# Moving the end of self-attention into cross-attention's first steps, and splitting the experts' weight loads, in a one-core decoder layer

## The reference

```
x = x + bitlinear(self_attention(quantised q, k, v of layernorm(x)), wo, go)
x = x + cross_attention(layernorm(x), context)         # 16 heads of 128, q and k rms-normalised
x = x + experts(layernorm(x))                          # 8 experts, top 2, 688 hidden, silu gate

bitlinear(x, w, g): x/rms(x)*g rounded to 8 bits per token, w rounded to -1, 0, 1
experts: probs = softmax(top 2 of x @ router_w.T)
         y = (silu(x @ gate.T) * (x @ up.T)) @ down.T, summed over the two with probs
```

## Time and profile before

| | us |
|---|---|
| median of 3 runs | 933.92 (932.38 to 935.29) |
| the profiled execution | 935.83 |
| its span, first to last instruction | 934.0 |
| PE busy | 792.0 (85%) |
| DVE busy | 628.4 (67%) |
| ACT busy | 537.2 (58%) |
| POOL busy | 385.2 (41%) |

### The profile page before, as it was taken

How to read it: one execution, slowest core, us unless ns; L and a number is a source line. 1 busy time by engine, 2 the same in 40 slices (tenths; PEclk the granted TensorE clock), 3 DMA queues, 4 the chain that set the end, 5 groups by cost and what they waited for, 6 DMA issues and landing times. The chain is left out here.

```text
span 934.0 us, 29446 instructions
## 1 busy us (share of the span) xinstructions
PE 792.0 (85%) x11809; PEld 574.7 (62%) x11809; DVE 628.4 (67%) x1110; ACT 537.2 (58%) x1002; POOL 385.2 (41%) x445
## 2 busy tenths in 40 slices
PE   0599989982998999999999969973989999999992
PEld 0488878861444656566656557651657777777771
DVE  6788999644789999989999989679323333333330
ACT  1687777762777767676767646340435445454450
POOL 0232222131346555555555575102344555555532
PEclk9998999965999999999999998985999999999996
DMA  9110000000463344434343522290682222222224
GB/s 323 52 49 25 26 25 26 26 2 26 145 208 121 119 133 136 123 109 137 93 138 104 157 90 65 71 385 15 253 277 45 41 41 46 37 44 44 38 35 107
DMA packets 59402, 91.97 MB, mean 98 GB/s; under 512 B 6768, under 2 KB 39664, under 8 KB 59088
## 3 DMA queue, kind: packets, MB, share of 16 engines
q1 hardware_dynamic: 48048, 76.26, 24.6%
q0 software_dynamic: 7488, 10.23, 6.8%
q10 hardware_dynamic: 3744, 3.67, 1.1%
HBM read 63.13 MB, written 29.10 MB: 99 GB/s over the span
## 5 line engine op out<-in xcount | busy, mean ns | idle before, releaser
L1565 DVE SCALAR_TENSOR_TENSOR hid<-psu,hid 128x688 f32<-128x688 f32 x39 | 34.1, 875 | 147.4 <-ACT hid L1427 147.4
L1178 PE MATMUL xbank_a<-arena,x_o 128*128 128x256 f16 x768 | 97.9, 279 | 8.5 <-DVE x_o L1003 6.1
L1427 ACT ACTIVATE hid<-psg 128x688 f32<-128x688 f32 x39 | 29.0, 744 | 117.3 <-PE psu L1642 117.3
L1178 PEld LDWEIGHTS xbank_a<-arena,x_o 128*128 128x128 f16 x768 | 72.3, 99 | 29.3 <-DVE x_o L1003 17.4
L1083 PE MATMUL xbank_qk<-arena 128*128 128x512 f16 x336 | 83.5, 385 | 5.0 <-DVE x_gains L988 3.9
L1657 PE MATMUL fbank<-arena,hidT 128*128 (+1 forms) x663 | 84.3, 276 | 0.8 <-ACT f_y L1447 0.8
L849 POOL TENSOR_TENSOR x_pf<-x_sc,x_rden 128x512 f32<-128x512 f32 x32 | 33.4, 1043 | 107.2 <-DVE x_rden L1026 107.2
L1642 PE MATMUL psg<-wgu,f_xT 128*128 x468 | 75.2, 310 | 2.1 <-ACT f_xT L1434 2.1
L1642 PE MATMUL psu<-wgu,f_xT 128*128 x468 | 74.6, 309 | 0.0
L1657 PEld LDWEIGHTS fbank<-arena,hidT 128*128 128x128 f16 (+1 forms) x663 | 63.5, 98 | 16.3 <-issue 9.5
L889 ACT ACTIVATE sqq<-xbank_qk 128x512 f32<-128x512 f32 x56 | 33.4, 597 | 64.5 <-PE xbank_qk L1083 64.5
(11 more groups left out here) (274 smaller groups left out, 2039.8 us busy)
## 6 DMA issues: line engine op xcount, KB each, us to landing
arena<-in_wx SPq DMA_DIRECT2D x51, 256.0 KB, 3.8
wgu<-w_hl SPq DMA_DIRECT2D x8, 1376.0 KB
ao<-key_norms SPq DMA_DIRECT2D x64, 128.0 KB, 3.7
w_hl<-cT SPq DMA_DIRECT2D x26, 256.0 KB, 2.1
w_hl<-x_pair SPq DMA_DIRECT2D x25, 256.0 KB, 3.3
arena<-w_hl SPq DMA_DIRECT2D x8, 384.0 KB
ao<-in_wx SPq DMA_DIRECT2D x10, 256.0 KB, 3.5
w_hl<-ao SPq DMA_DIRECT2D x10, 256.0 KB, 2.6
```

The lines of the kernel that those rows point to most:

```text
L1178: last = nc.tensor.matmul(acc[t // 2][:, (t % 2) * C:(t % 2 + 1) * C], o_hl[h % 2][:, a, at:at + P], wvo[:, b, e, :], start=(e == 0 and j ...
L1565: nc.vector.scalar_tensor_tensor(out=h3, in0=psu[:, :].rearrange("p (c n) -> p c n", c=2)[:, :, 0:FH], scalar=HID_UP / (H_UP * W_UP), in1= ...
```

## The change

Self-attention's loop now ends at t = 15. What was left of pairs 4 to 7 is done in the cross-attention block: a first part ahead of its loop, the rest between the operations of m = 0 to 6. The banks are cross-attention's own, `xbank_s` for turns of zo, the two halves of `xbank_o` for the projection and the turned pairs. The operands (ao2, ug, zo, zoT, hp, h, w_int and others, the tuple `Carry`) lie in slots of k_hl that heads of m = 5 to 8 write first, wvT_raw in slots 0 to 7. `value_weights` and its two splits go from lag 2 to lag 1, so to odd t = 1 to 15. PE's wait for the gains is gone, and ACT's explicit load of its table.

In the experts, SP loads the router's weights first, then the gate and up halves of all eight experts in two DMAs, then saves x, then loads the down weights of three experts; those of the other five wait for the routing. `gate_up` waits only for both gate and up DMAs; `down` waits for its expert.

```diff
-        steps = range(-4, NT + 7)
+        steps = range(-4, NT)
...
-                    if pair(t, 2) is not None:
-                        value_weights(t, pair(t, 2))
+                    if pair(t, 1) is not None:
+                        value_weights(t, pair(t, 1))
...
+                gained_last()
+                rest_low(5)
                 for N in steps:
-                    n = N + 1
+                    n, m = N + 1, N + AHEAD
                     if piece(piece_at(N, 1)):
                         piece_low(piece_at(N, 1))
+                    if m == 3:
+                        rest_low(6)
+                    if m == 5:
+                        rest_low(7)
...
-                nc.scalar.preload_act_table_set("natural_log_exp_and_others")
-                act.wait_ge(g_ready, 4)
...
+                def rest_high(j):
+                    act.wait_ge(h_done, 2 * (j - 4))
+                    act.wait_ge(ht_done, j - 4)
+                    nc.scalar.copy(hp[:, :, 0, :], h_rest[:, :, :]).then_inc(hh_done, 1)
...
+                squares_last()
+                second_norm(5)
+                turned_out(6)
+                rest_high(5)
+                quantise_last()
+                act.wait_ge(g_ready, 3)
...
                     if pair(m):
                         key(2 * m + 1)
+                    if m == 1:
+                        turned_out(7)
+                        second_norm(6)
+                    if m == 2:
+                        rest_high(6)
+                    if m == 3:
+                        second_norm(7)
+                    if m == 4:
+                        rest_high(7)
...
+                second_stats(5)
...
+                turned_hidden(4)
+                hidden(5)
+                scale_last()
+                dve.wait_ge(g_in, 32)
...
                     if pair(m):
                         query_low(2 * m)
                         key_halves(2 * m)
+                    if m == 0:
+                        integers_last()
+                    if m == 1:
+                        second_stats(6)
+                    if m == 2:
+                        hidden(6)
+                    if m == 3:
+                        second_stats(7)
+                    if m == 4:
+                        hidden(7)
...
                     if pair(m):
                         key_halves(2 * m + 1)
+                    if m == 0:
+                        residual_out(6)
+                    if m == 1:
+                        turned_hidden(5)
+                    if m == 2:
+                        residual_out(7)
+                    if m == 4:
+                        turned_hidden(6)
+                    if m == 6:
+                        turned_hidden(7)
...
-                pe.wait_ge(g_ready, 4)
...
+                turn_hidden(4)
+                turn_out(6)
...
                         key(2 * m)
+                    if m == 0:
+                        project_rest(6)
+                    if m == 1:
+                        turn_out(7)
+                    if m == 2:
+                        project_rest(7)
+                    if m == 4:
+                        turn_hidden(6)
+                    if m == 6:
+                        turn_hidden(7)
...
                     if pair(m):
                         squares(2 * m + 1)
+                    if m == 0:
+                        turn_hidden(5)
...
+                sp.dma_start(wr[:, :, :], dram["wr"].rearrange("p (k e) -> p k e", k=NCH)).then_inc(s["wr_in"], 16)
+                for l in range(2):
+                    sp.dma_start(wgu[:, :, l * GUC:(l + 1) * GUC], weights[l, :, :, 0:GUC]).then_inc(s["gate_up_in"], 16)
...
+                down_weights(0, 3)
+                sp.wait_ge(down_in[0], 64)
+                sp.sem_inc(s["experts_in"], 3)
+
+                sp.wait_ge(s["h_saved"], 32)
+                sp.wait_ge(s["routed"], 1)
+                down_weights(3, NE)
...
-                    pe.wait_ge(s["experts_in"], e + 1)
+                    if n == 0:
+                        pe.wait_ge(s["gate_up_in"], 32)
...
                     e = expert_of[n]
+                    pe.wait_ge(s["experts_in"], e + 1)
```

More of the change, by code:

```diff
@@ L2 @@
 from concourse import mybir
+from collections import namedtuple
 from contextlib import ExitStack
@@ L504, in _ @@
                         turned_hidden(pair(t, 8))
-                    if pair(t, 2) is not None:
-                        value_low(pair(t, 2))
+                    if pair(t, 1) is not None:
+                        value_low(pair(t, 1))
                     if tile(t + 1):
@@ new lines, in quantise_last, with turned_out @@
+                def quantise_last():
+                    act.wait_ge(so_done, 2)
+                    for a in range(2):
+                        nc.scalar.activation(ug[:, a, :], ug[:, a, :], ACT.Identity, scale=qsc_o[:, NPAIRS - 1, a:a + 1], bias=cst[:, CONSTS + 5:CONSTS + 6]).then_inc(yo_done, 1)
+                def turned_out(j):
+                    act.wait_ge(zt_done, j - 5)
+                    need(act, wo_done, j - 6)
+                    nc.scalar.copy(zoT[:, :, :, :].rearrange("p a k n -> p (a k n)"), bank_s[:, :].bitcast(BF16)[:, 0:2 * C]).then_inc(zoT_done, 1)
@@ new lines, in integers_last, with residual_out @@
+                def integers_last():
+                    dve.wait_ge(yo_done, 2)
+                    dve.wait_ge(zt_done, 1)
+                    nc.vector.tensor_scalar(zo[:, :, :], ug[:, :, :], MAGIC, None, ALU.subtract).then_inc(zo_done, 1)
+                def residual_out(j):
+                    dve.wait_ge(wo_done, j - 5)
+                    if j == NPAIRS - 1:
+                        dve.wait_ge(so_done, 2)
+                    for a in range(2):
+                        nc.vector.scalar_tensor_tensor(out=x_sb[:, 2 * j + a, :], in0=bank_wo[:, a * C:(a + 1) * C], scalar=deq_o[:, j, a:a + 1],
+                                                       in1=x_sb[:, 2 * j + a, :], op0=ALU.mult, op1=ALU.add).then_inc(xo_done, 1)
@@ new lines, in second_stats, with hidden @@
+                def second_stats(j):
+                    need(dve, xo_done, 2 * (j - 5))
+                    for a in range(2):
+                        c.step(nc.vector.bn_stats(stats_o[:, a, :], x_sb[:, 2 * j + a, :]))
+                    c.settle()
+                    for a in range(2):
+                        nc.vector.bn_aggr(mv_o[:, j, a, :], stats_o[:, a, :]).then_inc(st_done, 1)
+                def hidden(j):
+                    dve.wait_ge(rs_done, j - 4)
+                    dve.wait_ge(st_done, 2 * (j - 4))
+                    need(dve, hh_done, j - 5)
+                    need(dve, hl_done, j - 5)
+                    for a in range(2):
+                        nc.vector.tensor_scalar(h_rest[:, a, :], x_sb[:, 2 * j + a, :], mv_o[:, j, a, 0:1], rstd_h[:, j, a:a + 1], ALU.subtract, ALU.mult).then_inc(h_done, 1)
@@ L1361, in _, with down_weights @@
-                sp.wait_ge(w_in[(NE - 1) % 2], NE // 2 * 80)
-                sp.sem_inc(s["experts_in"], 1)
+                weights = dram["w_hl"].rearrange("l p (e n) -> l p e n", n=EC)
+                tail = (FT - 1) * C
+                def down_weights(first, end):
+                    part = slice(first, end)
+                    sp.dma_start(wd[:, part, 0:tail], weights[0, :, part, GUC:GUC + tail]).then_inc(down_in[first > 0], 16)
+                    sp.dma_start(wd[:, part, DC:2 * DC], weights[1, :, part, GUC:EC]).then_inc(down_in[first > 0], 16)
+                    for l in range(2):
+                        sp.dma_start(wd[l * S:l * S + S, part, tail:DC], weights[l, 0:S, part, GUC + tail:EC]).then_inc(down_in[first > 0], 16)
```

174 lines of the change are left out of this document (118 added, 56 removed).

## The result

| us | before | changed |
|---|---|---|
| median of 4 runs | 934.15 (932.38 to 935.29) | 924.79 (920.14 to 925.28) |
| the profiled execution | 935.83 | 920.14 |
| its span, mean granted clock | 934.0, 0.939 | 918.3, 0.952 |

The ratio is 0.989 (0.9859 to 0.9921): 9.4 us less by the medians, 15.7 by the profiled executions. So the time fell by about 1%, which is clear of the noise. The profiled execution of before is slower than all four in the table, that of the changed kernel is the fastest on record: five others took 921.55 to 925.63 us at granted clocks of 0.938 to 0.949. 0.943 instead of 0.952 is 17 us more at the half clock (time at the half clock is twice one minus the granted clock, times the stretch), so the clock alone can make 4 us between two executions of one kernel; that it did is an argument, not a test.

What follows compares the result with a forecast made beforehand. Bounds: TensorE and VectorE in self-attention, a tail filling no engine, TensorE in cross-attention's first steps, DMA among the experts. -21.2 + 6.0 + 6.0 - 5.2 = -14.4: 921.4 us profiled, 919.5 median; own range 912 to 927, also 910 to 928.

Steps and rivals of the forecast that it cites:

- term 2: Self-attention: value_weights one step earlier, from even to odd t, costs +6.0 us, ends -2 and +9.7.
- term 3: Cross-attention: the tail's work now standing at its start and in its steps costs +6.0 us, ends 3.9 and 10.7.
- Term 1: Seam after self-attention: the tail goes, the next block starts once t = 15 is done, -21.2 us.
- the four steps between: Self-attention's odd steps between t = 3 and 13, VectorE as full as TensorE: about 0.2 us each for value_weights.
- the prediction's own list of signs: Expected in the profile after, for self-attention: odd steps about 1 us longer, even ones unchanged, wait for pT near 2.9.
- 3 us more than fit: Cross-attention's steps: VectorE gets 7.1 us of moved work against 4 us of usable slack over seven steps.
- cross waits: Cross-attention's steps: engines waiting in order for each other, such as ScalarE's copy behind VectorE's normalising; 2.1 us taken.
- Term 4: Experts: with fewer weights loaded behind the routing, the stall in one expert's slot goes, -5.2 us.
- the fear of 3.9 us at the first gather: Experts: loads still in the air at 649 make the first gather take 7.93 instead of 4.04; rival's chance 0.06.
- the hiding: Rival, self- and cross-attention: moved work hides, term 2 at 0, term 3 at 3.9; 911.4 us; chance 0.15.
- non-hiding case: Rival, self- and cross-attention: term 2 and term 3 at their upper ends, sum -6.0, 928 us; chance 0.14.
- the slow rival: Cross-attention's steps: TensorE stays at the half clock, 941 us if half of them, 960 if all; chance 0.03.

Runs made afterwards that it cites:

- e3: The kernel before with only value_weights and its two halves one step earlier, at odd t: 941.94 us, ratio 1.0083 to before.
- e1: The changed kernel with value_weights back in the even steps, the eighth left in t = 15: 914.83 us, ratio 0.9794 to before.
- e4: The changed kernel with ScalarE's second_norm(7) moved from the end of m = 3 to behind the first key of m = 4: 921.67 us, ratio 0.9877 to before.
- e2: The kernel before with only the changed kernel's load order for the experts: 931.22 us, ratio 0.9953 to before.
- e6: e1 with POOL's low split half moved behind key_scale of the next even step, the gain behind it: 923.16 us, ratio 0.9875 to before.
- e10: The changed kernel with the value_weights products of t = 1 to 13 made twice: 921.76 us, ratio 0.9854 to before.
- e7: e1 with ScalarE's first copy of the turned probabilities ahead of squares and turned_out: 916.18 us, ratio 0.9812 to before.
- e8: The changed kernel with the edits of e1, e4, e6 and e7 together: 915.7 us, ratio 0.9794 to before.
- e9: e1 with each even step's value_weights products made twice: 910.64 us, ratio 0.9735 to before.
- e12: e9 with e4's move and the last split at t = 14 instead of t = 15: 910.8 us, ratio 0.9742 to before.

## Why the prediction was right, and where not

The time, 924.79, lies in the range (in both that the prediction names, 912 to 927 and 910 to 928) and 5.3 us above the forecast. For an execution like the profiled one 921.4 was forecast and 920.14 came. Of what was to be seen, the last split at 213 to 214 came at 217.45, just short of the 218 named as refuting; the scores at about 270 came at 271.04, and no slot is above 7 us. That the sum is so near is in part luck: term 2 was 3.6 us too small, term 3 was 2.8 too large, and 1.7 came in a stretch that had no term.

**Term 1** and **term 2** together: −15.2 forecast, −11.6 measured. That the next block starts with POOL's last split was right. Term 2 was too small: 6.0 for 9.6 (e3, alone: 8.7; e1, undone: 7.6). The step that failed is the 0.2 us taken for each of the four steps between, "where VectorE is as full". The odd steps with a clock of 0.96 or more in both kernels, t = 1, 5, 7, 11 and 13, became 0.75 to 1.06 us longer, the middle ones nearly as much as the ends, which is what the prediction's own list of signs said and its sum did not. I had asked what limits the odd step, and not what value_weights had covered in the even one: "TensorE idles behind it anyway" was true, but it also idles ahead of turn_out once the products are gone. The waits of an even step became 0.96 + 2.02 = 2.98 us, the 2.9 that I had named, with 0.96 of it at another instruction; and over the seven even steps TensorE's idle time went from 13.7 to 19.4 us and its time at the half clock from 12 to 30. In the odd steps it fell from 19 to 8 meanwhile, so over the stretch it rose only from 31 to 38. That clock had no place in the sum; how much of the 3.6 us is its doing no run separates. t = 15, at 2.0, was about right: e1, which keeps only that one, ends its last split at 209.88, 2.0 us later than before, 1.5 of them behind outputs(14).

**Term 3** was too large, 6.0 for 3.2 (the scores' start less the block's end: 53.6 for 50.4). The start gave 0.7 instead of costing 1.0: up to the end of m = 0 (the second squares at 226.90) it is 9.45 us, before 10.16, since TensorE's first queries lie beside the chain. The steps cost 3.9: 0.66 in m = 1, 0.45 each in m = 2 and 6, and 2.3 in m = 4. VectorE's 7.1 us were 6.7, with 0.9 more for pair 7's integers and the means of the statistics, which the list had left out; all of it fitted (19.07 of 20 us busy from 240 to 260, normalising at 406 ns a piece as in the tail, so no meeting with POOL there). The step that failed here is "3 us more than fit". The cross waits, which I had priced as a lump, were one wait, of ScalarE for the statistics of pair 7, and e4 takes 1.9 us of it away by moving two instructions.

**Term 4** was right: 5.2, by e2 alone 4.4 (3.1 to 5.7). The front did what was computed (full until about 640, ten microseconds of the shift included), and the fear of 3.9 us at the first gather was not borne out: 4.11 us with the load just ending. Router weights: 10.13 at the block's start and 10.21 at the first gather, so 0.1.

Between scores and experts another 1.7 us came, in the part that the change doesn't touch: 6 us at the half clock in 320 us where before had 13. I take it for an execution's chance (e2, with the old self-attention, also shows 0.99 there where before has 0.98); no run tests it.

The rivals: the hiding and the non-hiding case each came true for one term; the half clock of the slow rival showed neither in the steps (1.00 from m = 1 on) nor for long at the start (0.76 up to the end of m = 0, 4.5 us at the half clock); what more there was came in self-attention, which no rival named.

## What to carry to other kernels

Before moving an instruction out of a waiting stretch, ask which wait it was covering: look at the instruction behind it and at when that one's other input is ready. An operation may cost nothing where it is and about its whole time elsewhere, while nothing comes back. Before taking a collision between two engines away by moving one instruction, look at what the moved one will meet: in e6 half of the loss only changed places. And where one engine fills odd steps and others the even ones, price a move over the pair of steps, and let the experiment decide: two estimates by single steps here (the gain of e6, the cost of e10) were off by 6 us and more.

## What the runs showed of the hardware

- In t = 6, 8, 10 and 12 of the changed kernel TensorE runs at the half clock behind waits of 0.96 and 2.02 us a few microseconds apart: the products behind them take 1.97 us instead of 1.15. Shorter waits are no guarantee (e7, e8: less idle time, 36 and 43 us at the half clock instead of 27). With more work in the idle time the clock was higher in e9 and e12 (0.93 for 0.91). Which pattern is granted the full clock I can't say from these runs.
- The executions of one kernel differ by 2.5 to 9.5 us. In the changed kernel the order nearly follows the mean granted clock (920.14 at 0.952, 921.55 at 0.949, 925.28 at 0.938); in e12 it does not (906.18 at 0.956, 909.02 at 0.960), nor in e6 (915.02 at 0.952, 924.48 at 0.950).
- A VectorE tensor_scalar on three columns takes 1.71 us when it meets a POOL instruction of 2.13 us, and 0.23 when it doesn't; a scalar_tensor_tensor 1.09 and 0.20. e6 takes the meeting away and both fall, while a tensor_scalar on 768 columns that now meets POOL rises from 0.56 to 1.34. By that the trace agrees with the Trainium skill (SBUF — State Buffer, "Who interferes with whom"), by which a VectorE instruction in a two-port mode, or one with two inputs in SBUF beside a GpSimd instruction that reads SBUF, and that GpSimd instruction exclude each other. The 2.4 us a step were worth nothing here.
